# An expert tile's input, fetched by SyncE in 32x32 blocks and turned by VectorE instead of TensorE

## What is computed

```python
x = x + layernorm(attn(layernorm(x)))    # a Mamba-like scan: 512 channels, 16 states
x = x + layernorm(ffn(layernorm(x)))     # mixture of experts
# ffn, for each token x of width 256:
logits = x @ gate_w                      # 8 experts
top_v, top_i = top_k(logits, 2); top_p = softmax(top_v)
d_e = (silu(x @ Wg[e]) * (x @ Wu[e])) @ Wd[e]        # Wg, Wu: 256x704, Wd: 704x256
out = sum over the two chosen e of top_p * d_e  +  (silu(x @ Sg) * (x @ Su)) @ Sd
```

## Time and profile before

| | |
|---|---|
| median of three runs | 1716.26 us |
| the profiled execution | 1713.8 us, span 1712.0 us |
| TensorE busy | 88% of the span |
| VectorE busy | 79% |
| ScalarE, GpSimd busy | 58%, 61% |
| mean granted TensorE clock | 0.956 of full |
| expert tiles | from about 1120 to 1673 us of the span |
| last norm, residual and output | the rest, to 1712 us |

### The profile page before, as it was taken

How to read it: one execution, slowest core, us unless ns; L and a number is a source line. 1 busy time by engine, 2 the same in 40 slices (tenths; PEclk the granted TensorE clock), 3 DMA queues, 4 the chain that set the end, 5 groups by cost and what they waited for, 6 DMA issues and landing times.

```text
span 1712.0 us, 23925 instructions
## 1 busy us (share of the span) xinstructions
PE 1500.3 (88%) x6642; PEld 996.5 (58%) x6642; DVE 1353.0 (79%) x2425; ACT 1000.6 (58%) x1977; POOL 1043.6 (61%) x1233
## 2 busy tenths in 40 slices
PE   5888699899999998998998668699999999999990
PEld 2355455555655655745655555467677777777760
DVE  2199999899999899999899998256576676676665
ACT  3456667667668668659668564334454454454454
POOL 0478869979979879879889886312222322322224
PEclk9889899999999999999999968799999999999995
DMA  3011111311211221221211752523322222222216
GB/s 114 32 50 38 50 43 51 108 46 51 81 62 38 82 56 38 85 59 36 83 51 44 232 166 73 169 51 75 91 38 35 37 37 36 36 38 36 37 30 202
DMA packets 84398, 116.23 MB, mean 68 GB/s; under 512 B 11120, under 2 KB 58576, under 8 KB 84272
## 3 DMA queue, kind: packets, MB, share of 16 engines
q1 hardware_dynamic: 63344, 82.94, 16.0%
q0 software_dynamic: 16704, 27.57, 8.3%
q10 hardware_dynamic: 4224, 4.19, 0.7%
HBM read 81.05 MB, written 33.10 MB: 67 GB/s over the span
## 4 chain that ended last, share of the span: by engine, by line
PE 33%; POOL 6%; DVE 5%; issue 5%; ACT 2%; DMA 1%; SPq 0%; POOLq 0%; DVEq 0%; ACTq 0%
PE A L1244 10%; PE bA L1213 10%; PE bH L1213 10%; POOL arena L1018 4%; DVE arena L861 2%; DVE arena_t L878 1%; PE A L1235 1%; POOL expert_in_scratch L1006 1%; PE A L521 1%; DMA arena_t<-expert_in_scratch 0%; PE bH L591 0%; DMA sum_scratch<-arena_t 0%; DVE arena L878 0%; PE A L554 0%; DVE hT L1267 0%
## 5 line engine op out<-in xcount | busy, mean ns | idle before, releaser
L1018 POOL TENSOR_TENSOR arena<-arena 128x512 f32<-128x512 f32 x512 | 643.9, 1274 | 101.7 <-DVE arena L861 99.3
L735 ACT ACTIVATE bA<-arena,a_neg 128x512 f32<-128x512 f32 x512 | 352.1, 691 | 258.8 <-DVE arena L861 242.2
L591 PEld LDWEIGHTS bH<-ident,arena 128*128 128x128 f32 x2048 | 247.3, 146 | 303.0 <-DVE arena L861 139.3
L591 PE MATMUL bH<-ident,arena 128*128 128x128 f32 x2048 | 326.3, 287 | 93.9 <-DVE arena L861 72.9
L861 DVE TENSOR_TENSOR_SCAN arena<-bA,arena 128x512 f32<-128x512 f32 x256 | 305.7, 1210 | 63.6 <-ACT bA L735 48.8
L861 DVE TENSOR_TENSOR_SCAN arena<-bA,hl,arena 128x512 f32<-128x512 f32 x256 | 321.5, 1271 | 3.8 <-ACT bA L735 2.0
L1277 ACT COPY hT<-arena_t 32x160 f32<-32x160 f32 x568 | 182.5, 321 | 77.3 <-DVE arena_t L1261 71.6
L1267 DVE STREAM_TRANSPOSE hT<-arena_t 32x192 f32<-32x192 f32 x568 | 205.9, 363 | 6.6
L1371 POOL DMA_INDIRECT sum_scratch<-arena_t x71 | 113.5, 1598 | 148.6 <-issue 119.6
L1244 PE MATMUL A<-arena,hT 128*128 x852 | 197.5, 382 | 2.1 <-DVE hT L1267 2.1
L1365 POOL DMA_DIRECT2D arena_t<-expert_in_scratch x71 | 40.6, 573 | 257.5 <-issue 257.5
(11 more groups left out here) (191 smaller groups left out, 2042.0 us busy)
## 6 DMA issues: line engine op xcount, KB each, us to landing
arena<-b_scratch SPq DMA_DIRECT2D x128, 256.0 KB, 3.2
arena_t<-expert_in_scratch POOLq DMA_DIRECT2D x71, 132.0 KB, 2.4
arena<-in_L_ffn_Wg_dram SPq DMA_DIRECT2D x8, 704.0 KB
arena<-in_L_ffn_Wu_dram SPq DMA_DIRECT2D x8, 704.0 KB
arena<-in_L_ffn_Wd_dram SPq DMA_DIRECT2D x8, 640.0 KB
arena<-in_L_attn_x_dram SPq DMA_DIRECT2D x8, 512.0 KB, 5.1
arena_x<-in_L_attn_x_dram SPq DMA_DIRECT2D x8, 512.0 KB, 5.1
x_scratch<-arena_x SPq DMA_DIRECT2D x8, 512.0 KB, 3.2
```

The costliest lines, as they stand in the source:

```text
L591: i = e.transpose(bH[g % NH][:, q * P:(q + 1) * P], hh[:, (n - 1) % 2, q, d * P:(d + 1) * P], ident[:])
L735: e.activation(bA[g % NA][:], dt[c % 2][:, d, :], ACT.Exp, scale=a_neg[:, d, n:n + 1]).then_inc(s_a, 1)
L1018: e.tensor_tensor(bb[:, k % NB, :], u[c % 2][:, d, :], br[:, n % NR, :], ALU.mult).then_inc(s_bb, 1)
```

## The change

SyncE now fetches an expert tile. It does so in nine DMAs: eight carry 32 columns of all 128 rows each. Such a strip is four blocks of 32x32, and they land side by side on 32 partitions, the ones on which these 32 columns must stand once the tile is turned. A ninth DMA carries the eight extra numbers of each row. One VectorE instruction then turns all blocks of the tile in place of TensorE's turn and ScalarE's copy. Every wait for a fetched tile now counts 9 x 16. The fetch still waits for the scatter of the tile four before. GpSimd keeps only the scatters. SyncE's load of `x1` moves behind the fetch of tile 12 (`E + NX`).

```diff
+NIN = KD * (P // BLK) + 1
...
-    def pe_turn_in(e, t):
-        e.wait_ge(s_in[t % NX], 16 * (t // NX + 1))
-        if t:
-            e.wait_ge(s_kx, t)
-        for k in range(KD):
-            i = e.transpose(bX[:, k * P:(k + 1) * P], xt[:, t % NX, k * P:(k + 1) * P], ident[:])
-        i.then_inc(s_tx, 1)
...
+    def sp_fetch(e, t):
+        if t >= NX:
+            e.wait_ge(s_kx, t + 1 - NX)
+            e.wait_ge(s_gt, t + 1 - NX)
+            e.wait_ge(s_ys, 16 * (t + 1 - NX))
+        row = e.value_load(tab[0:1, 1, t:t + 1], min_val=0, max_val=SPARE + (E - 1) * P)
+        for q in range(P // BLK):
+            for k in range(KD):
+                e.dma_start(xt[q * BLK:(q + 1) * BLK, t % NX, k * P:(k + 1) * P].rearrange("j (a i) -> j a i", i=BLK),
+                            xs_d[bass.ds(row, P), k * P + q * BLK:k * P + (q + 1) * BLK].rearrange("(a j) i -> j a i", j=BLK)).then_inc(s_in[t % NX], 16)
+        e.dma_start(xt[:, t % NX, DM:RW], xs_d[bass.ds(row, P), DM:RW]).then_inc(s_in[t % NX], 16)
+
+    def fetched(e, t):
+        e.wait_ge(s_in[t % NX], 16 * NIN * (t // NX + 1))
+
+    def dve_turn_in(e, t):
+        fetched(e, t)
+        if t >= 2:
+            e.wait_ge(s_gu, t - 1)
+        e.transpose(xtT[:, t % 2, :, :].rearrange("p k q -> p (k q)"), xt[:, t % NX, 0:DM]).then_inc(s_kx, 1)
...
     def sync_tiles(e):
         pad_rows(e)
         e.wait_ge(s_x1s, 16 * NCH)
         e.wait_ge(s_shs, 16 * NCH)
+        e.wait_ge(s_tab, 1)
+        e.wait_ge(s_z, 16 * (E + 1))
+        e.wait_ge(s_padd, 16 * E)
         e.wait_ge(s_sc, 16 * J * TOPK * NCH)
-        e.wait_ge(s_dn, E)
-        for u in range(NU):
-            e.dma_start(x1s[:, u, :, :], unit_rows(x1_d, u)).then_inc(s_x1u, 16)
+        for t in range(NT):
+            sp_fetch(e, t)
+            if t == E + NX:
+                for u in range(NU):
+                    e.dma_start(x1s[:, u, :, :], unit_rows(x1_d, u)).then_inc(s_x1u, 16)
...
     def pool_tiles(e):
...
-                row = e.value_load(tab[0:1, 1, n:n + 1], min_val=0, max_val=SPARE + (E - 1) * P)
-                e.dma_start(xt[:, n % NX, :], xs_d[bass.ds(row, P), :]).then_inc(s_in[n % NX], 16)
...
     def act_tiles(e):
...
-                e.copy(xtT[:, (t + 1) % 2, :, :].rearrange("p k q -> p (k q)"), bX[:, 0:KD * P]).then_inc(s_kx, 1)
...
     def dve_tiles(e):
+        dve_turn_in(e, 0)
         for t in range(NT + 1):
             if t < NT:
                 dve_gate(e, t)
+            if t + 1 < NT:
+                dve_turn_in(e, t + 1)
```

More of the change, by code:

```diff
@@ L1184, in program @@
     gt = sb("gt", [P, 2])
-    bX, bG, bU, bD = A[0], bA, bH, [A[1], A[2]]
+    bG, bU, bD = bA, bH, [A[1], A[2]]
     s_wt = sem("s_wt")
     s_in = [sem(f"s_in{i}") for i in range(NX)]
-    s_tx = sem("s_tx"); s_kx = sem("s_kx"); s_g = sem("s_g"); s_gu = sem("s_gu"); s_si = sem("s_si"); s_h = sem("s_h")
+    s_kx = sem("s_kx"); s_g = sem("s_g"); s_gu = sem("s_gu"); s_si = sem("s_si"); s_h = sem("s_h")
     s_hb = sem("s_hb"); s_th = sem("s_th"); s_pl = sem("s_pl"); s_dn = sem("s_dn"); s_yt = sem("s_yt"); s_ys = sem("s_ys")
@@ L1350, in pool_tiles @@
     def pool_tiles(e):
[L1351 to L1363, removed]
-                row = e.value_load(tab[0:1, 1, n:n + 1], min_val=0, max_val=SPARE + (E - 1) * P)
-                e.dma_start(xt[:, n % NX, :], xs_d[bass.ds(row, P), :]).then_inc(s_in[n % NX], 16)
[L1366 to L1372, removed]
+        e.wait_ge(s_shs, 16 * NCH)
+        for t in range(NT):
+            fetched(e, t)
+            e.wait_ge(s_yt, t + 1)
+            if t:
+                e.wait_ge(s_ys, 16 * t)
+            e.indirect_dma_start(out=sh_d, out_offset=bass.IndirectOffsetOnAxis(ap=xt[:].bitcast(U32)[:, t % NX, TOK:TOK + 1], axis=0),
+                                 in_=yt[:, t % 2, :], in_offset=None, compute_op=ALU.add).then_inc(s_ys, 16)
         for u in range(NU):
@@ L1379, in pe_tiles @@
         e.wait_ge(s_tab, 1)
-        pe_turn_in(e, 0)
         ex = None
@@ L1392, in pe_tiles @@
                 pe_up(e, t, ex)
-            if t + 1 < NT:
-                pe_turn_in(e, t + 1)
             if t:
@@ L1398, in act_tiles @@
     def act_tiles(e):
-        for t in range(-1, NT + 1):
+        for t in range(NT + 1):
             if t >= 1:
                 act_place(e, t - 1)
-            if 0 <= t < NT:
+            if t < NT:
                 e.wait_ge(s_g, t + 1)
```

## The result

Four runs of the changed kernel took 1781.33 to 1785.06 us, median 1783.0, against 1714.45 for the kernel before (four runs). The ratio is 1.040, 95% interval 1.038 to 1.042. The profiled execution took 1782.66 us, 68.9 more than the 1713.8 of before; forecast were +80 and 1795.

The account below looks back on a forecast made before the run. TensorE alone was taken to bound the tiles before, a loop through the fetch after. Pace +71, first four tiles -1, start +10, x1 load 0 made +80 on 1713.8, stated as 1795 us, range 1745 to 1890.

Parts of the forecast that it names:

- The ring's trip: Expert tiles: loop from scatter through fetch, VectorE's turn, product and yt to the next scatter, 17.2 us for two tiles.
- The pace: Expert tiles: 8.6 us a tile against 7.54, 1.06 more from the fifth tile on, +71 us.
- The start: First fetch: SyncE waits for the shared expert's store, then issues nine DMAs; first gate later by 10 us.
- The x1 load: SyncE's load behind tile 12: delays the next fetch about as much as before, 0, between -5 and +8 us.
- TensorE's turn: Expert tiles: turning the input on TensorE goes away, 0.21 us a tile, 15 us over 71 tiles.
- VectorE's turn: Expert tiles: one 128x256 block turn added on VectorE, about 437 ns, by itself free.
- TensorE's clock: Expert tiles: TensorE 85% busy, clock costed at nothing; at clock 0.85 the 7.33 us become 8.6 and still hide.
- C: Rival, expert tiles: regular idling costs TensorE its full clock for long stretches, +100 over the forecast, 1895 us; chance 0.06.
- The signs: Expert tiles: gate waits 1 to 1.5 us nearly every tile, issues stretch some 4 us, tile 8.6, first gate near 1133.
- The range: Whole kernel: 1745 to 1890 us; all low ends together 1730, one low end about 1748.
- Rival A: Expert tiles: fetch stays hidden, issues and landing within 3.8 us in place of 6.3; about 1711 us; chance 0.08.
- rival B: Expert tiles: small-block fetch much dearer, through SyncE's price for runs (1970 us) or contention (1915 us); chance 0.18.

Follow-up runs that it names:

- e6: Changed kernel with the wait for the two stores moved from the first fetch to the x1 load: 1771.4 us, ratio 1.036 to the kernel before.
- e1: Changed kernel with five input buffers instead of four, x1 load still behind tile 12: 1698.7 us, ratio 0.995 to the kernel before.
- e2: Changed kernel with one 128x264 DMA a tile instead of nine, blocks not in their places: 1696.2 us, ratio 0.993 to the kernel before.
- e3: Changed kernel with three input buffers instead of four, x1 load still behind tile 12: 2320.1 us in one run.
- e7: Changed kernel with five buffers, no store wait ahead of the first fetch, x1 load in eight pieces: 1686.5 us, ratio 0.986 to the kernel before.
- e10: Changed kernel with the eight block DMAs made four of 256 runs each, other blocks fetched: 1749.8 us, ratio 1.021 to the kernel before.
- e5: Changed kernel unchanged, run again on another chip: 1780.2 us, ratio 1.042 to the kernel before.
- e8: Kernel before with only the x1 load cut into eight single pieces, one for every 6 tiles: 1700.8 us, ratio 0.995.
- e9: Changed kernel, four buffers, with the x1 load in eight pieces behind tiles 12, 18, 24 and so on: 1778.1 us, ratio 1.038 to the kernel before.

## Why the prediction was right

The mechanism was the forecast one, and the sizes were near, in part because misses cancelled. By its own steps:

- **The ring's trip**: 17.2 forecast, 16.87 measured, in the trip shown and as twice the mean pace. `yt` to scatter 0.77 and 0.73; landing 3.8 and 3.84; SyncE's wake and table load 0.86 and 0.80; eight issues 3.9 and 4.34; the ninth's landing 2.4 and 1.90; VectorE's turn to the product 0.54 and 0.37; product to `yt` 4.93 and 4.89. The two largest misses, +0.4 in the issues and -0.5 in the landing, cancel by luck. The row of eight static issues (0.49) was the right neighbour for an issue, 0.50; what it left out was 0.35 more ahead of the ninth. The landing came nearer to the low bound of 1.6 than to the 2.4 that I took.
- **The pace**: 8.6 forecast; 8.44 measured between 1265.85 and 1704.74 us (52 tiles). With the load of x1 it explains the +62.8: 68 x 0.90 = 61.2, and 1.5.
- **The start**: +10 forecast, +8.5 measured. e6 shows that it comes off the end in full, 8.7.
- **The x1 load**: 0 forecast (-5 to +8), +1.5 measured: 8.1 in the ring, 6.6 before.
- **TensorE's turn**: 0.21 us a tile forecast. e1 and e2, where the ring is slack, run at 7.32, 0.22 under before.
- **VectorE's turn**: 437 ns forecast, 445 measured.
- **TensorE's clock**: 0.97 to 0.98 between 1300 and 1700 us in the changed kernel, at 90% busy where 85% was forecast, so C came in hardly at all, and TensorE is not what the ring waits for. In e3 the same column shows 0.80 between 1500 and 1600 us, at 58% busy, and the gate in its rows takes 4.31 us instead of 2.53. The ring hides even that: from VectorE's turn to the next scatter it is 5.99 us there and 5.99 in the changed kernel.
- **The signs**: VectorE's turn waits for a DMA, SyncE issues over some 4 us, and a tile takes 8.4 us, as forecast. But TensorE's gate does not wait "in nearly every tile, by 1 to 1.5 us"; it waits in 28 of some 54, by 1.8 on average. The first gate came at 1129.23 and not near 1133, which is 2.9 from the shorter first stage and the rest from the start.
- **The range**: "with one low end it is about 1748" does not come out of the rows. The low end of the issues alone gives about 1764, that of the landing alone 1769, and the two together 1737.

The 68.9 measured are under the 80 forecast by three things: the pace gave 61 in place of 70, the start 1.5 less, and the first stage happened to be 2.9 shorter; the 1.5 of the load and rounding stand against it.

Rival A missed by far in the changed kernel: issues and landing took 6.2 us where it allowed 3.8. It is what e1, e2 and e7 then did, by a longer lead or fewer issues. Of rival B, the contention did not come: landing 1.9, scatter 3.8. But its price per run is real, as e10 shows, and it is the 2.2 ns that the prediction read from `b_dt`; it does not hide behind the 0.49 of an issue but is part of it, which at 128 runs an issue made no difference. On the one place where I set a figure of the Trainium skill beside a row ("DMA: Bandwidth & Descriptors", "Anatomy of one DMA": about 2.0 us fixed), I took it too widely. That section is about DMAs that GpSimd issues, and the ninth is SyncE's. For GpSimd's fetch of 132 KB the section's formula gives an estimate of 2.3 us, near the measured 2.4. The ninth DMA's 1.9 lies near the fixed part, but does not test it. The rule of the Trainium skill to join small transfers (same page, "Rules for kernel authors") held in direction: e2 is the same ring with one transfer in place of nine and is 4.5% faster than the changed kernel.

One thing that I had not seen: the rounds are uneven. VectorE waits 4.82 us for the fetch of one tile, in the rows above, and 0.90 for the next. Even and odd tiles are two rings side by side, and nothing spaces them evenly: the scatters of neighbours are about 6 and about 10.5 us apart in turn. The mean need not be free of this, as e10 shows. Its even stretch ran at 7.84 us a tile, with all 24 turns waiting for their DMA. In its uneven stretch, at 8.31, only 13 of 24 did, and many neighbours are some 5.8 us apart, like these:

```profile
1492.90 0.45 DVE L1295 STREAM_TRANSPOSE arena_t<-arena_t 128x256 f32<-128x256 f32 x1 [4.53 <-DMA arena_t<-expert_in_scratch]
...
1498.65 0.45 DVE L1295 STREAM_TRANSPOSE arena_t<-arena_t 128x256 f32<-128x256 f32 x1
```

The 5.75 us are VectorE's own round, back to back, so the second tile of such a pair waits for VectorE and not for its data. That this is what lengthens the trips is argued and not tested. How much the unevenness costs in the changed kernel was not measured.

One rival remedy was not run: VectorE's turn of t+1 placed behind the product of t, with four buffers and nine DMAs. In the trip shown the product could then start up to 4.3 us earlier, so it is the test that would show VectorE's order as a link by an experiment; so far it is shown by the trace alone.

## What to carry to other kernels

When a transfer waits for something that its own data brings about some steps later, add up the loop and divide by the number of steps that its buffers allow; a bound engine with 0% idle says nothing about how near that quotient is. Here 1.5 us of slack were spent on eight more issues, and the gain of 0.22 us a tile became a loss of 0.9; one more buffer gave it back. Before splitting a DMA into small ones, look for what the last of them is awaited by, and count the issues at their pitch, not at their length.

## What the runs showed that I had not expected

- SyncE's issue has a price per run beside its fixed price: start to start 0.50 us for 128 runs of 128 bytes (changed kernel) and 0.79 for 256 of them (e10), though the data engines are at 0.27 of their time.
- Nine times the runs a tile moved the DMA share only from 0.23 to 0.27 (the pace is slower too; at the pace of e1, 7.32, it is 0.32), and the scatter's landing stayed at 3.8 us. Only the small ninth DMA landed later at the quicker pace, 2.5 us in e1 and e7 against 1.7 in e5.
- Spreading 4 MB over eight single loads is free where the chain has slack (e7, e8). In the ring, which has none, it brought some 6 of the 8.1 us that the load in one go costs (e9).
